# Last node update of a two-layer graph kernel placed in the build banks, ahead of the last batch's products, with the end's loads begun four quads early

## The chip, the core and the metric

The kernel runs on one core of one Trainium2 chip. The metric is the device time of one execution in microseconds (us); the time before is the median of three runs. The core has a matrix engine (PE), a vector engine (DVE), a scalar engine (ACT), a general engine (POOL) and a queue-only engine (SP). SP, ACT and POOL issue DMAs. Each engine works through its own list in order, and semaphores join the lists.

## What is computed

Two graph layers over 6250 nodes with 64 features and 206250 edges sorted by destination. Cut to what matters:

```python
h = jnp.maximum(_layernorm(x, axis=-1), 0.0)
# layer 0: per edge relu([h[src], edge_attr] @ W1 + b1) @ W2 + b2, summed by dst;
#          per node relu([h, sum] @ U1 + c1) @ U2 + c2
x = x + _L0_gnn_ref(h, edge_index, edge_attr_64, ...)
h = jnp.maximum(_layernorm(x, axis=-1), 0.0)
# layer 1: segment_sum(h[src] * edge_weight, dst)
x = x + _L1_gnn_ref(h, edge_index, edge_weight)
```

## The kernel before, in words

**Groups.** The edges are cut into 202 groups of 1024. The main loop (fast_groups, one copy on each engine, all in the same steps s) does two things with group s. It sums layer 0: POOL gathers the rows, PE multiplies the edge features, DVE and ACT add and relu, PE sums by destination (sum_hid), and DVE adds the window to the node sums (add_sums, semaphore acc_added). And it builds layer 1's weighted adjacency as tiles: PE multiplies one-hot matrices into the two build banks pair[2] and pair[3] (build_tile), and ACT copies them into the tile buffer (keep_tiles, semaphore pair_kept). Two groups are a batch (101 batches, 0 to 100), four a quad (51 quads, 0 to 50; the last has one batch). SP stores each batch's tiles in HBM (store_adjacency). The last chunk's columns go to a tensor of their own, tail.

**Node update.** The nodes are ten chunks of 625. When a chunk's layer-0 sums are complete, PE makes g (make_g, two halves), ACT relus it (relu_g), PE makes the update (make_up), DVE adds it (add_up) and normalises it again with ACT's help (centre, square, variance, root, stage_h2; semaphore h2_staged). Chunk 9's sums are complete only with group 201, the last. Before, all of its steps go through mid_bank, a bank that late products share.

**Products.** Layer 1 multiplies the updated nodes h2 by the adjacency. direct(b, half) does it for batch b from the tiles in SBUF, with the chunks that are ready. ACT copies the result (keep_partial, semaphore direct_kept) and SP stores it in partial. late() does the same from pieces read back out of HBM (late_piece), through mid_bank, and DVE adds them up (keep_late) for SP to store (store_late). What is left over, chunk 9 for every quad and chunk 8 too for quads 36 to 46, is done at the end (fast_end).

**The end.** SP loads per quad the sum so far (load_partial, L644, 96 KB, into s_back) and a piece of 480 KB from tail (load_piece, L651) or from adjacency (L653). s_back has four slots: the load of quad q+4 waits until DVE has used quad q (u_kept). The ten slots for pieces lie in the tile buffer. PE multiplies a quad (multiply, L1266 and L1272), DVE adds the sum (keep_u, L1671), PE transposes it (turn_u, L1280), ACT copies, PE places it among the nodes (put, L1290), DVE adds (L1692). After every five quads PE turns a finished chunk (turn_sums, L1298), and it is written out.

**Order.** It is written by hand in each engine's loop. Before, PE does in step 201 direct(99, 1) and the last two late products, in step 202 direct(100, 0) and g's first half, in step 203 direct(100, 1) and g's second half, and in step 204 make_up. SP waits in fast_end, before the first load, for all stores of all kinds.

A float32 matmul is two passes in the profile, so its count there is twice that in the program's order.

Of the kernel before, what the change touches and what calls it, by code (L numbers as in the profile page):

```python
# [15 lines left out]
D = 64  # L16
# [5 lines left out]
NP = 125  # L22
BLK = 5
CN = NP * BLK
BC = BLK * D
# [91 lines left out]
def build(nc, x, src, dst, edge_attr, edge_weight, w1, b1, w2, b2, u1, c1, u2, c2, out):  # L117
# [79 lines left out]
        return sum(ready_for(i) > 0 for i in range(b + 1))  # L197

    ENDS = QUADS + 1

    def groups_of(q):

# [36 lines left out]
    with ExitStack() as ctx:  # L239
# [141 lines left out]
        sum_bank = mid_bank[:, 2 * QCOLS:2 * QCOLS + 2 * W]  # L381
        build_pair = [pair[2], pair[3]]
        assert max(SPLIT * NP, BC, 2 * QCOLS) <= 2 * QCOLS and 2 * QCOLS + 2 * W <= 512
        end_bank = [pair[3][:, 1, 0:2 * COLS], pair[3][:, 0, 0:2 * COLS]]
        turn_bank = [pair[2][:, 0, 0:2 * P], pair[0][:, 1, 0:2 * P]]
        add_bank = [pair[2][:, 1, 0:2 * WB], pair[0][:, 0, 0:2 * WB]]
# [182 lines left out]
        def _(sp):  # L569
# [67 lines left out]
            def store_late(n, q):  # L637
                sp.wait_ge(late_kept, n + 1)
                sp.dma_start(sums_of(2 * q, 2), late_sum[n % BACK]).then_inc(late_stored[n % BACK], 16)

            def load_partial(q):
                wait_count(sp, u_kept, q - SLOTS + 1)
                n = len(batches_of(q))
                sp.dma_start(s_back[:, q % SLOTS, 0:n * COLS], sums_of(2 * q, n)).then_inc(s_loaded[q % SLOTS], 16)  # L644

            def load_piece(q, n, c):
                slot, many = n % PIECES, groups_of(q)
# [12 lines left out]
            def fast_groups():  # L660
                for g in range(SLOTS):
                    load_ea(g, g % TWO)
                for s in range(GROUPS + 4):
# [12 lines left out]

            def fast_end():
                sp.wait_ge(direct_kept, direct_upto(BATCHES - 1))
                for half in range(STAGE // 2):
                    pairs = range(half, BATCHES, STAGE // 2)  # L680
                    sp.wait_ge(adj_stored[half], 16 * sum(has_body(b) for b in pairs))
                    sp.wait_ge(tail_stored[half], 16 * len(pairs))
                for s in range(2):
                    n = direct_upto(BATCHES - 1)
                    sp.wait_ge(s_stored[s], 16 * sum(i % 2 == s for i in range(1, n + 1)))
                for s in range(BACK):
                    sp.wait_ge(late_stored[s], 16 * len(range(s, len(LATE_STEP), BACK)))
                for q in range(ENDS):
                    load_partial(q)
                    for i, c in enumerate(chunks_left(q)):  # L690
                        load_piece(q, FIRST_PIECE[q] + i, c)

            def store_t2(c, slot):
                wait_step(sp, h2_staged, c)
# [121 lines left out]
        def _(act):  # L816
# [99 lines left out]
            def relu_g(c, half):  # L916
                cols = (0, SPLIT * NP) if half == 0 else (SPLIT * NP, CN)
                act.wait_ge(g_made, 2 * c + half + 1)
                wait_count(act, up_made, c)
                act.activation(t_stage[0:D, 0, cols[0]:cols[1]], mid_bank[0:D, 0:cols[1] - cols[0]],  # L920
                               ACT.Relu).then_inc(g_staged, 1)

            def clear_sums(c):
# [5 lines left out]
            def fast_groups():  # L929
                act.wait_ge(table_turned, 20)  # L930
                keep_turned_ea(0, 0)
                keep_turned_ea(1, 1)
                for s in range(GROUPS + 6):
# [12 lines left out]
                    for c in range(CHUNKS):  # L946
                        if s == SUMMED[c]:
                            relu_g(c, 0)
                        if s == SUMMED[c] + 1:
                            relu_g(c, 1)  # L950
                        if s == SUMMED[c] + 2:
                            clear_sums(c)
                        if s == SUMMED[c] + 3:
                            square(2)(c, 0)
                        if s == SUMMED[c] + 4:
                            root(2)(c, 0)

            def keep_turned(q):
                n = len(batches_of(q)) * P
# [44 lines left out]
        def _(pe):  # L1004
# [192 lines left out]

            def make_g(c, half):
                cols = (0, SPLIT * NP) if half == 0 else (SPLIT * NP, CN)
                if half == 0:  # L1200
                    wait_count(pe, late_kept, late_by(SUMMED[c]))
                    pe.wait_ge(acc_added, min(SUMMED[c] + 1, GROUPS))
                    wait_count(pe, x1_made, c)
# [1 line left out]
                    pe.wait_ge(g_staged, 2 * c + 1)  # L1205
                    pe.wait_ge(acc_added, min(SUMMED[c] + 2, GROUPS))
                for w, of in ((u1_deg, beside), (w2u_twice, sums1)):
                    last = pe.matmul(mid_bank[0:D, 0:cols[1] - cols[0]], w[:, :],
                                     of[:, c * CN + cols[0]:c * CN + cols[1]], start=(w is u1_deg),
                                     stop=(w is w2u_twice))  # L1210
                last.then_inc(g_made, 1)

            def make_up(c):
                pe.wait_ge(g_staged, 2 * c + 2)
                pe.wait_ge(acc_added, min(SUMMED[c] + 3, GROUPS))
                for b in range(BLK):
                    last = pe.matmul(mid_bank[0:NP, b * D:(b + 1) * D], t_stage[:, 0, b * NP:(b + 1) * NP],
                                     u2_s[:, :], start=True, stop=True)
                last.then_inc(up_made, 1)

            def fast_groups():
# [4 lines left out]
                for s in range(GROUPS + 6):  # L1226
# [14 lines left out]
                    b = s // 2 - 1  # L1241
                    if 0 <= b < BATCHES and ready_for(b):
                        direct(b, s % 2)
                    late(s)
                    for c in range(CHUNKS):
                        if s == SUMMED[c]:
# [6 lines left out]
            def multiply(q):  # L1253
                bank, many = end_bank[q % 2], groups_of(q)
                wait_count(pe, u_kept, q - 1)
                for i, c in enumerate(chunks_left(q)):
                    n = FIRST_PIECE[q] + i
                    slot = n % PIECES
# [119 lines left out]
        def _(dve):  # L1378
# [254 lines left out]
                        dve.tensor_copy(to, of).then_inc(late_kept, 1)  # L1633

            def fast_groups():
                for s in range(GROUPS + 6):
                    if 1 <= s <= GROUPS:
                        add_sums(s - 1)
                    if s < GROUPS:
# [14 lines left out]
                    for c in range(CHUNKS):  # L1654
# [4 lines left out]
                            variance(2)(c, 0)  # L1659
                        if s == SUMMED[c] + 5:  # L1660
                            stage_h2(c, 0)

            def keep_u(q):

# [123 lines left out]
```

## Time and profile before

| what | us |
|---|---|
| median of 3 runs | 2261.81 |
| lowest, highest run | 2261.12, 2263.18 |
| the profiled execution's own time | 2270.83 |
| its span, first to last instruction | 2269.0 |
| PE, DVE, POOL, ACT busy in the span | 1797.8, 1632.2, 1613.5, 842.8 |
| mean granted clock of PE | 0.931 of full |

The profiled execution takes 1.83 us more than its span, and 9.0 us more than the median of the runs. Times inside the trace are microseconds from the span's start. "The chain" is the chain of work that ended last, followed back from the last instruction.

### The profile page before, as it was taken

How to read it: one execution, taken by the hardware profiler on the slowest of the kernel's cores; microseconds unless marked ns; L12 is line 12 of the kernel's file. 1: busy time of each engine (PE TensorE's matmuls, PEld its weight loads, DVE VectorE, ACT ScalarE, POOL GpSimd, SP SyncE). 2: the span in 40 equal slices, each digit the busy share in tenths (PEclk: the TensorE clock that was granted, in tenths of full speed). 3: DMA queues.
4: the chain of work that ended last, by engine and by line, in shares of the span. 5: the costliest groups of instructions: out<-in, count | busy, mean ns of one | idle time of the engine just before them, and what ended most of it. 6: DMA issues, size and time to landing. Idle time of an engine off the chain costs nothing.

```text
span 2269.0 us, 52026 instructions
## 1 busy us (share of the span) xinstructions
PE 1797.8 (79%) x19448; PEld 1527.7 (67%) x19448; DVE 1632.2 (72%) x4933; ACT 842.8 (37%) x1470; POOL 1613.5 (71%) x1671
## 2 busy tenths in 40 slices
PE   6766576767677777778778877888888899999898
PEld 6555455655565666567667766776777788788787
DVE  7876677767776777777777777777777677877564
ACT  5333343434343434333343333434334333433211
POOL 7777777777777777777777777777777777777200
PEclk9988889878998999899989999999999999999999
DMA  4355556555764676378548755875876588578798
GB/s 104 113 179 178 179 176 204 185 172 173 241 208 137 197 249 209 112 232 255 187 129 260 247 159 165 255 227 156 248 234 197 170 268 257 154 218 255 228 304 278
DMA packets 375605, 459.58 MB, mean 203 GB/s; under 512 B 77256, under 2 KB 297688, under 8 KB 371766
## 3 DMA queue, kind: packets, MB, share of 16 engines
q1 hardware_dynamic: 317274, 401.51, 53.7%
q0 software_dynamic: 51776, 53.07, 10.3%
q8 instruction: 160, 2.62, 0.5%
q10 hardware_dynamic: 6300, 1.60, 0.3%
q14 instruction: 95, 0.78, 0.1%
HBM read 281.45 MB, written 174.54 MB: 201 GB/s over the span
## 4 chain that ended last, share of the span: by engine, by line
POOL 67%; issue 21%; PE 8%; DMA 3%; DVE 1%; ACT 0%; SPq 0%; POOLq 0%
POOL rows L780 67%; PE pair L1266 2%; PE pair L1046 1%; DMA stage<-tail 1%; DMA late_piece<-adjacency 1%; PE pair L1162 1%; PE pair L1290 1%; PE pair L1180 1%; PE pair L1147 1%; PE pair L1280 1%; DMA stage<-adjacency 0%; PE pair L1034 0%; PE pair L1298 0%; DMA rows<-table,idx 0%; PE pair L1272 0%
## 5 line engine op out<-in xcount | busy, mean ns | idle before, releaser
L780 POOL DMA_INDIRECT rows<-table,idx x1616 | 1574.2, 974 | 494.6 <-issue 492.4
L906 ACT COPY stage<-pair 128x600 f32<-128x600 f32 x808 | 538.7, 667 | 882.3 <-PE pair L1147 837.7
L1147 PE MATMUL pair<-bld 128*128 128x300 bf16 x4848 | 757.6, 309 | 5.7 <-DVE bld L1599 5.6
L1147 PEld LDWEIGHTS pair<-bld 128*128 128x128 bf16 x4848 | 549.0, 118 | 140.9 <-issue 14.0
L1599 DVE TENSOR_SCALAR bld<-iota_key,key 128x300 bf16<-128x300 f16 x1616 | 583.0, 361 | 78.1 <-PE pair L1147 75.9
L1609 DVE TENSOR_TENSOR bld<-bld,part 128x512 bf16<-128x512 bf16 x1212 | 481.6, 397 | 0.0
L1107 PE MATMUL pair<-w1b,rings 128*128 128x128 f32 x1616 | 258.2, 310 | 253.3 <-DVE rings L1575 252.9
L1575 DVE TENSOR_TENSOR rings<-rows,pair 128x512 f32<-128x512 f32 x202 | 138.9, 688 | 427.9 <-DMA rows<-table,idx 424.4
L1107 PEld LDWEIGHTS pair<-w1b,rings 128*128 128x128 f32 x1616 | 227.6, 216 | 289.0 <-DVE rings L1575 286.6
L1180 PE MATMUL pair<-late_piece,h 125*64 125x192 f32 x1856 | 201.9, 337 | 117.2 <-issue 104.6
L1162 PE MATMUL pair<-stage,h 125*64 125x96 f32 x4230 | 234.8, 253 | 0.2 <-issue 0.2
L1180 PEld LDWEIGHTS pair<-late_piece,h 125*64 125x64 f32 x1856 | 133.4, 138 | 138.7 <-issue 132.2
L1162 PEld LDWEIGHTS pair<-stage,h 125*64 125x64 f32 x4230 | 204.9, 140 | 0.7 <-issue 0.6
L896 ACT ACTIVATE rings<-rings 128x512 f32<-128x512 f32 x202 | 127.6, 632 | 191.4 <-DVE rings L1575 191.3
L1602 DVE TENSOR_TENSOR bld<-iota_lo,lo 128x512 bf16<-128x512 f16 x404 | 161.7, 400 | 0.0
L1592 DVE TENSOR_REDUCE hot_sum<-hot 128x40 f32<-128x320 f32 x202 | 156.6, 775 | 7.0
L1134 PE MATMUL pair<-hot,rings 128*64 128x40 f32 x3232 | 136.2, 233 | 24.5 <-DVE x_all L1614 23.9
L1134 PEld LDWEIGHTS pair<-hot,rings 128*64 128x64 f32 x3232 | 112.6, 139 | 59.7 <-issue 59.7
L1100 PE MATMUL pair<-ident,rings 128*128 128x128 f32 x808 | 125.7, 280 | 2.5 <-issue 1.7
L892 ACT COPY rings<-pair 128x512 f32<-128x512 f32 x202 | 118.9, 588 | 10.8 <-PE pair L1100 10.7
L1100 PEld LDWEIGHTS pair<-ident,rings 128*128 128x128 f32 x808 | 102.7, 146 | 7.5 <-issue 2.0
L1579 DVE TENSOR_TENSOR hot<-iota,rel 128x320 f32<-128x320 f32 x202 | 98.9, 490 | 0.0
(155 smaller groups left out, 1120.8 us busy)
## 6 DMA issues: line engine op xcount, KB each, us to landing
late_piece<-adjacency SPq DMA_DIRECT2D x232, 480.0 KB
rings<-in_edge_attr_dram SPq DMA_DIRECT2D x202, 256.0 KB
adjacency<-stage SPq DMA_DIRECT2D x14, 2160.0 KB
rows<-table,idx POOLq DMA_INDIRECT x1616
tail<-stage SPq DMA_DIRECT2D x101, 240.0 KB
stage<-tail SPq DMA_DIRECT2D x50, 480.0 KB, 5.8
adjacency<-stage SPq DMA_DIRECT2D x10, 1920.0 KB
adjacency<-stage SPq DMA_DIRECT2D x10, 1680.0 KB
```

The source lines that it names most:

```text
L780: pool.indirect_dma_start(out=rows[:, slot, t, :], out_offset=None, in_=table, in_offset=bass.IndirectOffsetOnAxis(ap=idx[:, g, t:t + 1], ...
L906: act.copy(tiles[:, g % STAGE, :, 2 * j * WT:2 * (j + 1) * WT].rearrange("p h (o w) -> p o h w", w=WT), build_pair[i % 2][:, :, 0:KEYS].re ...
L1100: last = pe.transpose(bank[:, a * P:(a + 1) * P], ea_ring[:, slot, a * P:(a + 1) * P], ident[:, :])
L1107: last = pe.matmul(bank[:, a * P:(a + 1) * P], eaT[:, slot, a, :], w1b2[:, :], start=True, stop=True)
L1134: pe.matmul(half_of(sum_bank, t)[:, 0:W], hid[:, slot, t, 0:D], hot[:, slot, t, :], start=(t < 2), stop=(t >= T - 2))
L1147: last = pe.matmul(build_pair[i // 2 % 2][:, t % 2, 0:KEYS], hot_w[q % 2][k][:, :, u], hot_key[q % 2][:, u, :], start=(k == 0), stop=(k == ...
L1162: last = pe.matmul(half_of(u_bank, h), h2[:, h * D:(h + 1) * D], tiles[0:NP, slot:slot + 2, h, :], start=(h < 2), stop=(h >= many - 2))
L1180: pe.matmul(half_of(mid_bank, h)[:, at:at + QCOLS], h2[:, (c * BLK + h) * D:(c * BLK + h + 1) * D], held[:, :, h, :], start=(h < 2), stop= ...
L1592: dve.tensor_reduce(hot_sum[:, g % TWO, :], hot[:, g % TWO, :, :].rearrange("p t w -> p w t"), AX_X, ALU.add).then_inc(hot_summed, 1)
L1599: return dve.tensor_scalar(hot_key[q % 2][:, u, :], iota_key[:, :], key[:, g, t + u:t + u + 1], None, ALU.is_equal)
L1602: dve.tensor_tensor(hot_eq[q % 2], iota_lo[:, :, :], over(lo[:, g, t:t + 4], P), ALU.is_equal).then_inc(eq_made, 1)
L1609: dve.tensor_tensor(hot_w[q % 2][k], hot_eq[q % 2], over(part[k][:, g, t:t + 4], P), ALU.mult)
```

## The change

It concerns the last three steps and the end. The update of chunk 9 no longer goes through mid_bank but through pair[2], a build bank, and it is written into step 201 on PE: both halves of g straight after direct(99, 1), then direct(100, 0), make_up, direct(100, 1) and only then the two late products. DVE takes the update before the last two keep_late, ACT takes keep_partial(100) after root. On SP the one wait for all stores is split up: for the first four quads it waits for the stores of odd batches and the quad's own sum, loads them ahead of the stores of batch 100's and the last late sums, and then waits quad by quad. The pieces rotate by five slots, so that the first five lie where batch 99's tiles were and not batch 100's.

```diff
+        final_g = [pair[2][:, 0, :], pair[2][:, 1, :]]
+        final_up = pair[2][:, 0, :]
...
+            def piece_slot(n):
+                return (n + PIECES // 2) % PIECES
...
             def load_partial(q):
                 wait_count(sp, u_kept, q - SLOTS + 1)
+                if q < QUADS and late_of[q]:
+                    n = late_of[q][-1]
+                    sp.wait_ge(late_stored[n % BACK], 16 * (n // BACK + 1))
...
             def fast_end():
-                sp.wait_ge(direct_kept, direct_upto(BATCHES - 1))
-                for half in range(STAGE // 2):
...
+                final = BATCHES - 1
+                store_adjacency(final)
+                store_partial(final - 1)
+                tiles_stored((final - 1) % 2)
+                for q in range(AHEAD):
+                    load_quad(q)
+                store_partial(final)
+                for n, c, q in LATE_AT[GROUPS - 1]:
+                    store_late(n, q)
+                tiles_stored(final % 2)
+                for q in range(AHEAD, ENDS):
+                    load_quad(q)
...
+                relu_g(FINAL, 0)
+                relu_g(FINAL, 1)
+                clear_sums(FINAL)
+                square(2)(FINAL, 0)
+                root(2)(FINAL, 0)
+                keep_partial(BATCHES - 1)
...
             def make_g(c, half):
                 cols = (0, SPLIT * NP) if half == 0 else (SPLIT * NP, CN)
-                if half == 0:
+                to = final_g[half] if c == FINAL else mid_bank
+                if c == FINAL:
+                    pe.wait_ge(pair_kept, TILES // 2)
+                    pe.wait_ge(acc_added, GROUPS)
+                elif half == 0:
...
+                    if s == GROUPS - 1:
+                        make_g(FINAL, 0)
+                        make_g(FINAL, 1)
+                        direct(BATCHES - 1, 0)
+                        make_up(FINAL)
+                        direct(BATCHES - 1, 1)
                     late(s)
...
+                add_sums(GROUPS - 1)
+                add_up(FINAL, final_up[0:NP, 0:BC])
+                centre(2)(FINAL, 0)
+                variance(2)(FINAL, 0)
+                stage_h2(FINAL, 0)
+                many = len(LATE_AT[GROUPS - 1])
+                keep_late(GROUPS - 1, 1 if many == 3 else 0, many)
```

FINAL is chunk 9, AHEAD is 4, ENDS is 51.

PE's list before, from the end of direct(99, 1) to the end of make_up. The x23 row is direct(99, 1), L1180 and L1185 are the two late products, L1162 direct(100, ...), L1208 g, L1217 make_up; pair1 holds mid_bank:

```order
L1162 MATMUL pair1<-stage,h2 64x96 x23
L1180 MATMUL pair1<-late_piece,h2 64x192 [waits h2_staged,acc_added,late_loaded0,x1_made,late_kept]
L1180 MATMUL pair1<-late_piece,h2 64x192 x3
L1185 MATMUL pair1<-late_piece,h2 64x96 x2
L1180 MATMUL pair1<-late_piece,h2 64x192 [waits late_loaded1,h2_staged]
L1180 MATMUL pair1<-late_piece,h2 64x192 x3
L1185 MATMUL pair1<-late_piece,h2 64x96 x2
L1162 MATMUL pair1<-stage,h2 64x96 [waits direct_kept,h2_staged,pair_kept]
L1162 MATMUL pair1<-stage,h2 64x96 x21
L1208 MATMUL pair1<-nodes,u1_deg 64x375 [waits x1_made,acc_added,late_kept]
L1208 MATMUL pair1<-nodes,w2u_twice 64x375
L1162 MATMUL pair1<-stage,h2 64x96 x23
```

The same place of PE's list in the changed kernel, from direct(99, 1) to the first late product (there L1193 is direct, L1243 g, L1253 make_up, L1211 a late product):

```order
L1193 MATMUL pair1<-stage,h2 64x96 x23
L1243 MATMUL pair2<-nodes,u1_deg 64x375 [waits acc_added,pair_kept]
L1243 MATMUL pair2<-nodes,w2u_twice 64x375
L1243 MATMUL pair2<-nodes,u1_deg 64x250 [waits acc_added,pair_kept]
L1243 MATMUL pair2<-nodes,w2u_twice 64x250
L1193 MATMUL pair1<-stage,h2 64x96 [waits direct_kept,h2_staged,pair_kept]
L1193 MATMUL pair1<-stage,h2 64x96 x21
L1253 MATMUL pair2<-u2_s,t_stage 125x64 [waits acc_added,g_staged]
L1253 MATMUL pair2<-u2_s,t_stage 125x64 x4
L1193 MATMUL pair1<-stage,h2 64x96 x23
L1211 MATMUL pair1<-late_piece,h2 64x192 [waits h2_staged,acc_added,late_loaded0,x1_made,late_kept]
```

The update moved ahead of batch 100's second half and of both late products, into another bank and without the wait for late_kept; no instruction came or went.

SP's list before, from the last store of tiles to the first loads of the end (L639 store_late, L614 store_partial, L644 and L651 the loads of a quad):

```order
L608 DMA tail<-stage 128x2x240 [waits pair_kept]
L614 DMA partial<-stage 128x96 [waits direct_kept]
L639 DMA partial<-late_own 128x192 [waits late_kept]
L639 DMA partial<-stage 128x192 [waits late_kept] x2
L614 DMA partial<-stage 128x96 [waits direct_kept]
L644 DMA bld<-partial 128x192 [waits late_stored0,s_stored1,late_stored1,s_stored0,late_stored2,tail_stored1,late_stored3,adj_stored1,late_stored4,tail_stored0,late_stored5,adj_stored0,direct_kept]
L651 DMA stage<-tail 128x960
```

SP's list at the same place in the changed kernel (L614 is now the tiles' store, L620 store_partial, L660 and L667 the loads of a quad, L645 store_late):

```order
L614 DMA tail<-stage 128x2x240 [waits pair_kept]
L620 DMA partial<-stage 128x96 [waits direct_kept]
L660 DMA bld<-partial 128x192 [waits late_stored4,tail_stored1,adj_stored1]
L667 DMA stage<-tail 128x960
L660 DMA bld<-partial 128x192 [waits late_stored5]
L667 DMA stage<-tail 128x960
L660 DMA bld<-partial 128x192 [waits late_stored0]
L667 DMA stage<-tail 128x960
L660 DMA bld<-partial 128x192 [waits late_stored1]
L667 DMA stage<-tail 128x960
L620 DMA partial<-stage 128x96 [waits direct_kept]
L645 DMA partial<-late_own 128x192 [waits late_kept]
```

Four quads' loads moved ahead of the last four stores.

## Rows read from the trace of the kernel before

**Rows 1.** The page: the whole chain by engine.

```profile
POOL 67%; issue 21%; PE 8%; DMA 3%; DVE 1%; ACT 0%; SPq 0%; POOLq 0%
```

**Rows 2.** The chain in order of time, 2128 to 2160: start, length, what.

```profile
2132.28 0.87 PE pair L1180 x8
...
2135.66 0.62 PE pair L1208 x2
...
2136.77 1.98 PE pair L1162 x44
2138.76 0.86 PE pair L1208 x4
...
2140.07 1.32 PE pair L1217 x10
...
2141.41 0.50 DVE x_all L1614
...
2158.67 0.80 PE pair L1266 x8
2159.47 0.17 PE pair L1272 x4
```

**Rows 3.** Timeline of PE, 2129 to 2170: start, length, operation [idle before, releaser].

```profile
2131.18 0.85 PE L1180 MATMUL pair<-late_piece,h 125*64 125x192 f32 x8
...
2145.39 1.55 PE L1266 MATMUL pair<-stage,h 125*64 125x192 f32 x8 [4.02 <-DVE h L1404]
...
2156.84 0.87 PE L1266 MATMUL pair<-stage,h 125*64 125x192 f32 x8 [1.63 <-DMA stage<-tail]
...
2160.37 0.87 PE L1266 MATMUL pair<-stage,h 125*64 125x192 f32 x8
...
2162.14 0.87 PE L1266 MATMUL pair<-stage,h 125*64 125x192 f32 x8
...
2164.95 0.87 PE L1266 MATMUL pair<-stage,h 125*64 125x192 f32 x8
```

**Rows 4.** Windows: length, busy PE, PEld, DVE, ACT, POOL, then clock, DMA share, GB/s.

```profile
2132.00:2134.00 2.00, 1.73 (x29) 1.38 (x26) 0.62 (x2) 0.00 (x0) 0.00 (x0) 1.00 0.69 217
...
2136.00:2138.00 2.00, 2.00 (x39) 1.70 (x39) 0.00 (x0) 0.48 (x1) 0.00 (x0) 1.00 0.02 3
...
2146.00:2148.00 2.00, 1.97 (x16) 1.34 (x14) 0.65 (x3) 0.00 (x0) 0.00 (x0) 0.50 1.02 374
```

**Rows 5.** Timeline of SP's queue: when a DMA was issued.

```profile
2131.69 0.32 SPq L614 DMA_DIRECT2D partial<-stage  x1
...
2141.31 0.42 SPq L651 DMA_DIRECT2D stage<-tail  x1
...
2148.10 0.43 SPq L651 DMA_DIRECT2D stage<-tail  x1
...
2158.66 0.43 SPq L651 DMA_DIRECT2D stage<-tail  x1
```

**Rows 6.** L651's landings: 2140 to 2212, then issues of 2141.3, 2148.1, 2149.95.

```profile
DMA to landing us min/median/max: 3.3/5.4/6.7
DMA to landing us min/median/max: 3.3/3.3/3.3
DMA to landing us min/median/max: 4.5/4.5/4.5
DMA to landing us min/median/max: 6.7/6.7/6.7
```

**Rows 7.** Timeline of DVE: the last late sums, the first quad's sum.

```profile
2133.36 0.74 DVE L1629 TENSOR_TENSOR stage<-pair,stage 128x192 f32<-128x192 f32 x2 [3.29 <-PE pair L1185]
...
2147.35 0.36 DVE L1671 TENSOR_TENSOR bld<-pair,bld 128x192 f32<-128x192 f32 x1 [1.38 <-PE pair L1272]
```

**Rows 8.** PE's waits from 2129 on, and the chain at quad 36.

```profile
PE pair L1266 <- DMA stage<-tail: 2.1, 3, 1.6
...
2218.62 1.99 PE pair L1266 x19
```

More of the change, by code:

```diff
@@ L199, in build @@
     ENDS = QUADS + 1
+    FINAL = CHUNKS - 1
+    AHEAD = 4
+    assert SUMMED[FINAL] == GROUPS and SUMMED[FINAL - 1] + GAP + 2 <= GROUPS and ready_for(BATCHES - 1)
+    assert AHEAD <= SLOTS and AHEAD <= PIECES // 2
     def groups_of(q):
@@ L639, in store_late @@
                 sp.dma_start(sums_of(2 * q, 2), late_sum[n % BACK]).then_inc(late_stored[n % BACK], 16)
+            def piece_slot(n):
+                return (n + PIECES // 2) % PIECES
             def load_partial(q):
                 wait_count(sp, u_kept, q - SLOTS + 1)
+                if q < QUADS and late_of[q]:
+                    n = late_of[q][-1]
+                    sp.wait_ge(late_stored[n % BACK], 16 * (n // BACK + 1))
+                else:
+                    for b in batches_of(q):
+                        i = direct_upto(b)
+                        sp.wait_ge(s_stored[i % 2], 16 * ((i + 1) // 2))
                 n = len(batches_of(q))
@@ L646, in load_piece @@
             def load_piece(q, n, c):
-                slot, many = n % PIECES, groups_of(q)
+                slot, many = piece_slot(n), groups_of(q)
                 wait_count(sp, piece_used, n - PIECES + 1)
@@ L662, in fast_groups @@
                     load_ea(g, g % TWO)
-                for s in range(GROUPS + 4):
+                for s in range(GROUPS):
                     if s % 2 == 0 and 2 <= s <= GROUPS:
@@ L675, in fast_groups, with load_quad, tiles_stored @@
                         load_late(n, c, q, q not in LATE_QUAD[:n])
-            def fast_end():
-                sp.wait_ge(direct_kept, direct_upto(BATCHES - 1))
-                for half in range(STAGE // 2):
[L680 to L691, printed above, removed]
+            def load_quad(q):
+                load_partial(q)
+                for i, c in enumerate(chunks_left(q)):
+                    load_piece(q, FIRST_PIECE[q] + i, c)
+            def tiles_stored(half):
+                pairs = range(half, BATCHES, STAGE // 2)
+                wait_count(sp, adj_stored[half], 16 * sum(has_body(b) for b in pairs))
+                sp.wait_ge(tail_stored[half], 16 * len(pairs))
+            def fast_end():
+                final = BATCHES - 1
[10 more added lines that the diff above has]
+                    load_quad(q)
             def store_t2(c, slot):
@@ L919, in relu_g @@
                 wait_count(act, up_made, c)
-                act.activation(t_stage[0:D, 0, cols[0]:cols[1]], mid_bank[0:D, 0:cols[1] - cols[0]],
+                of = final_g[half] if c == FINAL else mid_bank
+                act.activation(t_stage[0:D, 0, cols[0]:cols[1]], of[0:D, 0:cols[1] - cols[0]],
                                ACT.Relu).then_inc(g_staged, 1)
@@ L932, in fast_groups @@
                 keep_turned_ea(1, 1)
-                for s in range(GROUPS + 6):
+                for s in range(GROUPS):
                     if s < GROUPS:
@@ L1207, in make_g @@
                 for w, of in ((u1_deg, beside), (w2u_twice, sums1)):
-                    last = pe.matmul(mid_bank[0:D, 0:cols[1] - cols[0]], w[:, :],
+                    last = pe.matmul(to[0:D, 0:cols[1] - cols[0]], w[:, :],
                                      of[:, c * CN + cols[0]:c * CN + cols[1]], start=(w is u1_deg),
@@ L1215, in make_up @@
                 pe.wait_ge(acc_added, min(SUMMED[c] + 3, GROUPS))
+                to = final_up if c == FINAL else mid_bank
                 for b in range(BLK):
-                    last = pe.matmul(mid_bank[0:NP, b * D:(b + 1) * D], t_stage[:, 0, b * NP:(b + 1) * NP],
+                    last = pe.matmul(to[0:NP, b * D:(b + 1) * D], t_stage[:, 0, b * NP:(b + 1) * NP],
                                      u2_s[:, :], start=True, stop=True)
@@ L1225, in fast_groups @@
                 make_q(0, 0, q_bank)
-                for s in range(GROUPS + 6):
+                for s in range(GROUPS):
                     if s < GROUPS:
@@ L1257, in multiply @@
                     n = FIRST_PIECE[q] + i
-                    slot = n % PIECES
+                    slot = (n + PIECES // 2) % PIECES
                     pe.wait_ge(piece_loaded[slot], 16 * (n // PIECES + 1))
@@ L1635, in fast_groups @@
             def fast_groups():
-                for s in range(GROUPS + 6):
+                for s in range(GROUPS):
                     if 1 <= s <= GROUPS:
```

## Prediction, made before the changed kernel ran

> **What bounds the kernel now.** I read the page first, then the chain in order of time, then each engine's timeline from 2128 us on. The page says that the chain is POOL's gathers for two thirds of the span [rows 1]. The change touches nothing there: the gathers are over by 2132 (POOL's column is 0.00) [rows 4], and every list is the same up to direct(99, 1). So only the last 138 us can move, and the reader should see three things in them.
>
> First, the road to chunk 9's update. direct(99, 1) gives way to the late products at 2131.18 [rows 3]. The DVE addition of the update starts at 2141.41 [rows 2]. Between them lie 10.2 us of PE work in a row, of which the update needs only part. Second, the gap behind it: PE's first multiply of the end starts at 2145.39 after 4.02 us of idleness, and it is slow, 1.55 us for eight passes where later ones take 0.87 [rows 3]. The granted clock is 0.50 there, PE's lower level of 1.2 GHz, and was 1.00 at 2136 [rows 4]. Third, the DMA engines have almost nothing to do at 2136 to 2138 (share 0.02) [rows 4], because SP's first load of a piece goes out at 2141.31 only [rows 5]. Then they are full, and quad 5's piece comes late: PE stands for 1.63 us at 2156.84 [rows 3].
>
> After that the end is PE's. A quad takes 1.77 us (2160.37 to 2162.14) and one with turn_sums 2.81 (2162.14 to 2164.95), so a run of five takes 9.9 us and one quad 1.98 on average [rows 3]. All of its waits for tail pieces sum to 2.1 us, of which the one at quad 5 is 1.6 [rows 8].
>
> **The update's move.** PE now takes from 2131.2: g's first half, four passes at 0.31 (0.62 for two) = 1.24; the second half, 0.86 for four; direct(100, 0), 44 passes, 1.98 by the other half's row; make_up until DVE can add, 2141.41 - 2140.07 = 1.34 [rows 2]. The sum is 5.42, so DVE adds at 2136.6 instead of 2141.41: **4.8 us** earlier. What it has to wait for is there: its two semaphores stand for the last copy of a build bank and the last add_sums, and both follow products that stand ahead of direct(99, 1), which alone is longer than either. g's relus on ACT (0.48 us for the larger half, ACT's column at 2136 [rows 4]) lie beside direct(100, 0); without that cover the second would cost up to 0.48.
>
> From the addition to the first multiply it is 3.98 us (2145.39 - 2141.41), a chain of small DVE and ACT steps that stays as it is [rows 2, 3]. So h2 is there at 2140.6. PE is not idle meanwhile: after make_up (ten passes, issued by about 2136.3) come direct(100, 1) with 2.0 us and two late products of 1.1 us each, together 4.2, to 2140.5 (2132.28 - 2131.18 = 1.10 [rows 2, 3]). They cost nothing, because the chain of h2 covers them to within 0.1 us; if it did not, each would cost its 1.1. ACT's copy of batch 100's product now stands behind root and ends beside the two DVE steps that h2 needs after root, hidden too. On DVE the last late sums (0.74 us) now stand between h2 and the memset of the pads [rows 7]; for that and a small step behind it I put 0.65, an estimate from the 0.36 of the three-times smaller sum of a quad. They end at about 2142.0, and the sum of quad 0 can start there. By itself it could have started at 2141.8, when its multiply is over, so this costs 0.2 us.
>
> **The clock.** The idleness of 4.0 us is gone. In this trace the clock fell only behind it; 1.63 us of idleness at 2156.84 did not lower it (0.87 before and after) [rows 3]. So I take the first quads at the full rate: 0.97 us for quad 0 (0.80 + 0.17 [rows 2]), 1.24 for quad 1 with its transpose, which I put at 0.27, and 1.77 for each from quad 2 on.
>
> **The loads.** SP reaches the first load right after the store of 2131.69 [rows 5], so at 2132.1. All four quads are issued by 2136, when the DMA share is 0.69 and then nearly nothing [rows 4]. Even with the longest landing of 6.7 us [rows 6] quad 0's piece is there at 2139.2, before 2140.6. Four of the quads are thus paid in idle time. What is queued behind them on SP are four stores: they wait for direct_kept (about 2140) and late_kept (about 2141.5) and are out before 2142. Quad 4's load needs u_kept of quad 0, at 2142.5, so it is not held up. It is issued at 2142.9, 2.3 us after the first multiply.
>
> What is late next is quad 4. PE could start it 5.75 us after the first multiply. It starts at 2.3 + L4, where L4 is its piece's time to landing. Quad 8 then starts 1.82 + L8 after quad 4, where 1.82 is the time from a quad's multiply to the issue of the load that it lets go (2156.84 to 2158.66 [rows 3, 5]), or 4 x 1.77 = 7.08 after it if PE is slower. Before, quad 8 starts 2162.14 - 2145.39 = 16.75 after the first multiply. L4 is not in the trace. The nearest rows are 3.3 us for a first load on empty queues, 4.5 for quad 4 of before, 6.7 for one behind others [rows 6]. I take 4.5, since in the new kernel too a few small stores are in front of it. For L8 I take the median, 5.4. Quad 4 starts at 6.8 and quad 8 at 14.0, **2.75 us** earlier than by the old start. It holds the clock's part and the wait's part together.
>
> As to quad 4 the Trainium skill would have it otherwise. Its page "DMA: Bandwidth & Descriptors", section "Anatomy of one DMA — SWDGE (gpsimd) path", fits a DMA as about 2.0 us and the bytes at 436 GB/s. That is an estimate of 3.4 us for the 576 KB of a quad, though for another path than SP's; the first load of before, 3.3 us, agrees, while the 6.7 behind others does not. By it quad 4 would not wait at all, which is the rival "no wait" below.
>
> From quad 8 on everything is the old course, shifted, with quads 36 to 46 (two pieces each) too. Pieces in other slots move no more bytes, and I cost them nothing.
>
> **Sum.** 4.8 + 2.75 = 7.5 us. The profiled span would go from 2269.0 to 2261.5, and its own time from 2270.83 to 2263.3. None of this hangs on the profiler, so the median goes from 2261.81 to **2254.3 us**.
>
> **Rivals.**
> *Queue takes it back.* Both loads take 6.7 us: quad 4 starts at 9.0, quad 8 at 9.0 + 1.82 + 6.7 = 17.5, 0.8 later than by the old start. 4.8 - 0.8 = 4.0, so 2257.8. For it speaks that quad 5's load, issued while the first four were still arriving, took that long; against it, that the first four are now in before quad 4 is asked for.
> *No wait.* L4 is at most 3.45 us, L8 at most 5.26; PE alone sets quad 8, at 0.97 + 1.24 + 6 x 1.77 = 12.8. The gain is 3.9 + 4.8 = 8.7, so 2253.1. The first load of before with its 3.3 us speaks for it, the median 5.4 against it.
> *It doesn't do what it says.* The update is issued early but held, by the last copy of a build bank or by the late products that now fill PE up to h2. If the first multiply comes only 1 us earlier, what is left is that and the clock and load parts: 3.7, so 2258.1. The order of the lists speaks against it.
> *The ring of four turns too slowly.* PE now runs ahead without the old pauses. If landings grow, each round of four quads lasts 1.82 + L instead of 4 x 1.98 = 7.9. That decides from L = 6.1. With eight rounds from quad 4 to quad 36, and 2218.6 - 2145.4 = 73.2 us for that stretch before [rows 3, 8], a mean L of 7.0 gives 9.3 + 8 x 8.82 = 79.9. That is 6.7 lost against 4.8 gained: 2263.7, slower than before. From L = 6.8 it is slower at all. No single landing in the trace is above 6.7, and the change adds no bytes.
>
> **How the numbers follow.** Forecast 0.62, queue takes it back 0.13, no wait 0.19, doesn't do what it says 0.03, ring too slow 0.03. A measurement of this kernel can tell about 0.2% from no change, 4.5 us, so the bounds are 2257.3 and 2266.3. Faster: forecast, no wait and a little of the first rival, 0.82. Same: the rest of it, the third, and part of the fourth, 0.16. Slower 0.02. The range reaches from "no wait" to "queue takes it back", with half a microsecond beyond each for the runs' own spread (2261.12 to 2263.18): 2252.4 to 2258.3.
>
> **What would show it.** In the new trace: g in front of direct(100, 0) at about 2131.2; the addition of the update about 4.8 us earlier, counted from the last build product; no idleness above 1 us ahead of the first multiply, and 0.87 us for its eight passes at clock 1.00; loads from just after the store of batch 99's sum; a wait of about 1 us at quad 4 and nearly none at quad 5; the ninth quad's multiply 14.0 us after the first. The prediction is wrong if the first multiply is less than 4 us earlier, if the clock stays at 0.50 there, or if the end from quad 8 on is no longer the old one shifted, say with waits for pieces that sum to more than 3 us.

## The result, and the profile after

| | before | changed |
|---|---|---|
| median of 20 runs each, us | 2263.38 | 2257.16 |
| lowest, highest | 2259.59, 2268.59 | 2253.26, 2264.06 |
| ratio, 95% interval | 1 | 0.9973 (0.9966 to 0.9981) |
| span of the profiled execution | 2269.0 | 2253.2 |
| last group's sum to the end of the span | 140.27 | 131.70 |

The change gains 6.2 us, 4.3 to 7.7 by the interval (0.0019 and 0.0034 of 2263.4). The two spans differ by far more, 15.8 us. So I count from here on from one point in each trace, the start of the last group's sum on PE (the last L1134 product of before, at 2128.73, and L1165 after). Up to it the changed kernel is 7.2 us shorter, behind it 8.6. The timeline of PE in the changed kernel (start, length, operation, idleness before it and what ended it), from the sum to quad 8:

```profile
2121.50 0.67 PE L1165 MATMUL pair<-hot,rings 128*64 128x40 f32 x16
...
2133.35 0.87 PE L1308 MATMUL pair<-stage,h 125*64 125x192 f32 x8 [0.27 <-DVE h L1446]
...
2139.73 0.87 PE L1308 MATMUL pair<-stage,h 125*64 125x192 f32 x8 [0.47 <-DMA stage<-tail]
...
2142.12 0.87 PE L1308 MATMUL pair<-stage,h 125*64 125x192 f32 x8 [0.56 <-DMA stage<-tail]
...
2147.43 0.87 PE L1308 MATMUL pair<-stage,h 125*64 125x192 f32 x8
```

The first multiply comes 11.85 us after the sum, where before it came 2145.39 - 2128.73 = 16.66 after it. It takes 0.87 us where it took 1.55, and PE stood for 0.27 us where it stood for 4.02 [rows 3]. Quads 4 and 5 wait for their pieces, 1.03 us together, and quad 8 starts 14.08 us after the first multiply.

The road there, by the chain in order of time. It answers [rows 2]: g (L1243), half of direct(100) (L1193), make_up (L1253), the other half, and on another view DVE's addition:

```profile
2124.16 1.83 PE pair L1243 x7
...
2128.09 1.23 PE pair L1253 x10
2129.33 2.04 PE pair L1193 x45
```

```profile
2129.36 0.49 DVE L1656 TENSOR_TENSOR x_all<-x_all,pair 125x320 f32<-125x320 f32 x1 [6.52 <-PE pair L1253]
```

SP's timeline shows the loads' new place, which answers [rows 5]. The store of batch 99's sum, the first piece 1.3 us behind it, and quad 4's piece:

```profile
2124.46 0.32 SPq L620 DMA_DIRECT2D partial<-stage  x1
...
2125.72 0.43 SPq L667 DMA_DIRECT2D stage<-tail  x1
...
2135.38 0.43 SPq L667 DMA_DIRECT2D stage<-tail  x1
```

The windows around the first multiply (columns as in [rows 4]: length, busy engines, clock, DMA share, GB/s) have the clock at 1.00, its upper level, throughout:

```profile
2132.00:2134.00 2.00, 1.73 (x25) 1.57 (x23) 1.54 (x6) 0.42 (x2) 0.00 (x0) 1.00 0.91 353
2134.00:2136.00 2.00, 2.00 (x28) 1.68 (x25) 1.91 (x8) 0.37 (x1) 0.00 (x0) 1.00 0.59 199
```

And PE's waits from 2125 on, which answer [rows 8]: 1.0 us for tail pieces in all, where before had 2.1.

```profile
PE pair L1308 <- DMA stage<-tail: 1.0, 2, 0.6
...
PE pair L1308 <- DVE h L1446: 0.3, 1, 0.3
PE pair L1308 <- DMA stage<-adjacency: 0.2, 1, 0.2
```

### The profile page after: what moved, and what is told of

The parts are those of the page before. It is cut to its first block, busy times and chain, and to the rows that moved or that the text cites. A ratio compares the mean times of both kernels' runs of the same rounds, so it can differ in the third digit from the quotient of the medians.

```text
span 2253.2 us, 52069 instructions
## 1 busy us (share of the span) xinstructions
PE 1788.3 (79%) x19448; PEld 1525.7 (68%) x19448; DVE 1638.4 (73%) x4933; ACT 842.4 (37%) x1470; POOL 1605.6 (71%) x1671
## 4 chain that ended last, share of the span: by engine, by line
POOL 65%; issue 21%; PE 10%; DMA 4%; DVE 1%; SPq 0%; ACT 0%; POOLq 0%
POOL rows L804 65%; DMA late_piece<-adjacency 2%; PE pair L1308 2%; PE pair L1193 1%; PE pair L1178 1%; PE pair L1211 1%; DMA stage<-tail 1%; PE pair L1077 1%; PE pair L1332 1%; PE pair L1322 1%; DMA stage<-adjacency 0%; PE pair L1340 0%; PE pair L1065 0%; PE pair L1165 0%; PE pair L1138 0%
## 5 line engine op out<-in xcount | busy, mean ns | idle before, releaser
L804 POOL DMA_INDIRECT rows<-table,idx x1616 | 1566.3, 969 | 494.6 <-issue 492.3
L1178 PEld LDWEIGHTS pair<-bld 128*128 128x128 bf16 x4848 | 547.8, 118 | 136.9 <-issue 12.9
L1211 PE MATMUL pair<-late_piece,h 125*64 125x192 f32 x1856 | 206.7, 343 | 120.6 <-issue 100.9
L1211 PEld LDWEIGHTS pair<-late_piece,h 125*64 125x64 f32 x1856 | 136.8, 141 | 142.6 <-issue 139.6
L1193 PE MATMUL pair<-stage,h 125*64 125x96 f32 x4230 | 233.1, 252 | 0.0
L1193 PEld LDWEIGHTS pair<-stage,h 125*64 125x64 f32 x4230 | 203.5, 139 | 0.2
L1165 PE MATMUL pair<-hot,rings 128*64 128x40 f32 x3232 | 135.4, 233 | 26.2 <-DVE x_all L1656 26.1
L1165 PEld LDWEIGHTS pair<-hot,rings 128*64 128x64 f32 x3232 | 111.8, 138 | 61.1 <-issue 61.1
```

The lines of the kernel that those rows point to most:

```text
L804: pool.indirect_dma_start(out=rows[:, slot, t, :], out_offset=None, in_=table, in_offset=bass.IndirectOffsetOnAxis(ap=idx[:, g, t:t + 1], ...
L1165: pe.matmul(half_of(sum_bank, t)[:, 0:W], hid[:, slot, t, 0:D], hot[:, slot, t, :], start=(t < 2), stop=(t >= T - 2))
L1178: last = pe.matmul(build_pair[i // 2 % 2][:, t % 2, 0:KEYS], hot_w[q % 2][k][:, :, u], hot_key[q % 2][:, u, :], start=(k == 0), stop=(k == ...
L1193: last = pe.matmul(half_of(u_bank, h), h2[:, h * D:(h + 1) * D], tiles[0:NP, slot:slot + 2, h, :], start=(h < 2), stop=(h >= many - 2))
L1211: pe.matmul(half_of(mid_bank, h)[:, at:at + QCOLS], h2[:, (c * BLK + h) * D:(c * BLK + h + 1) * D], held[:, :, h, :], start=(h < 2), stop= ...
```

## The experiments

All runs but the last (the third of the ring of six) were on chips on which the main loop took 820 to 880 us longer than above, in the kernel before as well (3145 instead of 2263 us), so that their ratios are wide. The gathers are not longer there (962 ns on average in the changed kernel's second trace, against 974 in the trace of before), but the mean granted clock of PE is lower, 0.81 against 0.93, and the chain runs over PE for half of the span. Why the clock is lower, no run told. The stretch behind the last group's sum was not touched by it: the changed kernel's first multiply is at 11.85 or 11.86 us in each of its four profiles, the one above among them. So the verdicts rest on positions in that stretch, one profile each, in us:

| kernel | sum to first multiply | first multiply to quad 8 | sum to the end |
|---|---|---|---|
| before, three profiles | 16.66, 17.16, 17.64 | 16.75, 15.65, 17.48 | 140.27, 140.14, 141.92 |
| changed, four profiles | 11.85, 11.86, 11.85, 11.85 | 14.08, 14.72, 14.57, 13.97 | 131.70, 132.69, 133.78, 131.85 |
| update only | 18.81 | 17.09 | 142.07 |
| loads only | 15.99 | 14.80 | 136.23 |
| loads only, gap filled | 16.31 | 14.06 | 136.76 |
| changed, through mid_bank | 12.70 | 14.12 | 133.34 |
| changed, ring of six, three profiles | 11.86, 11.86, 11.85 | 13.40, 12.90, 12.91 | 127.89, 127.50, 127.55 |

### The update without the early loads

The changed kernel with SP's old end:

```diff
-                for q in range(AHEAD):
-                    load_quad(q)
-                store_partial(final)
...
+                for s in range(BACK):
+                    sp.wait_ge(late_stored[s], 16 * len(range(s, len(LATE_STEP), BACK)))
+                for q in range(ENDS):
+                    load_partial(q)
```

> The changed kernel with SP's old end: PE, ACT and DVE take the update early, but SP waits for all stores before the first load, as before. Positions are counted from the start of the last group's sum (the last L1134 product of before, 2128.73 in its trace). Theory (the loads have to come early too, or the update's move is lost): the last late sums are now at about 12.5 us, their stores are issued by 13 and landed 2 us later, so the first load of a piece goes out at about 15 and lands 3.3 us later: the first multiply of the end comes at 18.5 us instead of 16.7 of before, behind 6 us of idleness of PE with the clock at its lower level. The end is 1 to 2 us longer than before, in all about 2264 where before is 2262.5. Rival (the update's road alone bounds the start of the end): the first multiply at 11.9 us and a gain of 4 to 5 us.

Measured: ratio 1.001 (0.999 to 1.003), and the first multiply 18.81 us after the sum. The timelines of SP (the last store, the first piece) and PE:

```profile
3015.19 0.44 SPq L620 DMA_DIRECT2D partial<-stage  x1
3017.20 0.32 SPq L660 DMA_DIRECT2D bld<-partial  x1
3017.57 0.43 SPq L667 DMA_DIRECT2D stage<-tail  x1
```

```profile
3021.14 1.54 PE L1300 MATMUL pair<-stage,h 125*64 125x192 f32 x8 [7.23 <-DMA stage<-tail]
```

h2 is ready early, but SP waits for the last stores to land, 2.0 us from the last issue, and the piece takes 3.3 more. PE stands for 7.23 us. The rival falls: without the loads the update's move gains nothing, and its end is 0.2 to 1.9 us longer than those of the kernel before.

### The loads without the update

The kernel before with the new fast_end, load_partial and piece_slot on SP, and the rotated slots on PE:

```diff
-                    slot = n % PIECES
+                    slot = (n + PIECES // 2) % PIECES
```

> The kernel before with SP's new end (four quads' loads early, quad by quad waits, pieces rotated by five); PE, ACT and DVE keep their old order. Theory: the first multiply stays at 16.7 us from the last group's sum, still behind 4.0 us of idleness and at the lower clock. Quad 4 and quad 5 no longer wait (1.63 us at quad 5 before), so quad 8 comes 15.1 us after the first multiply where before has 16.75: a gain of 1.6 to 2.1 us. Rival (the old course of the end is set by something else than late pieces, such as the clock): no gain, 0 to 0.5 us.

Measured: ratio 0.9995 (0.9977 to 1.0012). PE's first multiply and its waits for the rest of the span:

```profile
3035.56 1.55 PE L1285 MATMUL pair<-stage,h 125*64 125x192 f32 x8 [4.03 <-DVE h L1423]
```

```profile
PE pair L1285 <- DVE h L1423: 4.0, 1, 4.0
...
PE pair L1317 <- DVE nodes L1711: 0.4, 1, 0.4
PE pair L1285 <- DMA stage<-adjacency: 0.3, 1, 0.3
```

The idleness of 4.03 us and the slow first multiply stay, and not one tail piece is waited for. Quad 8 comes 14.8 us after the first multiply, as expected (15.1). The end is 3.9 to 5.7 us shorter than in the kernel before, more than the 1.6 to 2.1 I gave. Two things were missing in that sum. The later waits of before go too. And the first multiply comes at 15.99 us, not at the 16.7 I expected: before is late there, by 0.7 us in its first trace, and this edit changes nothing on PE ahead of it. That share is not the loads' gain; the section on the two kernels run again shows where it lies.

### The gap filled

The loads-only kernel with products that nobody reads in PE's idle time:

```diff
             def fast_end():
+                for _ in range(13):
+                    pe.matmul(pair[2][:, 0, 0:P], ident[:, :], ident[:, :], start=True, stop=True)
                 pe.wait_ge(twice_made, 1)
```

> The loads-only kernel (update in its old place, four quads' loads early) with 13 products of the identity with itself put on PE between make_up and the first multiply, into a bank that nobody reads; they fill most of the 4.0 us in which PE stood. They add nothing to the output. Theory (what the first quads lost was the clock, and the clock fell for the idleness): the granted clock stays at 1.00, the first eight passes take 0.87 us instead of 1.55, and the fourth quad starts 4.1 us after the first multiply instead of 6.0; the end is 1.5 to 2 us shorter than in the loads-only kernel (136.2 us from the last group's sum), if quads 4 and 5 don't wait instead. Rival (the first quads are slow for cold data or for their long waits on DVE): 1.55 us and 6.0 us again.

Measured: ratio 0.9986 (0.9965 to 1.0007). PE's timeline, with the filling products in the first row, and the window of the first multiply:

```profile
3014.96 3.12 PE L1323 MATMUL pair<-ident 128*128 128x128 f32 x26
3019.15 0.87 PE L1285 MATMUL pair<-stage,h 125*64 125x192 f32 x8 [1.07 <-DVE h L1425]
```

```profile
3018.00:3020.00 2.00, 0.93 (x14) 0.88 (x15) 1.32 (x4) 0.26 (x1) 0.00 (x0) 1.00 0.00 0
```

With the gap filled the clock stays at 1.00 and eight passes take 0.87 us. The fourth quad (quad 3) starts 4.07 us after the first multiply where the unfilled kernel has 5.96: 1.9 us, as expected, and the rival falls. In the loads-only kernel the window before the first multiply had stood at 0.50. But the end is no shorter, 136.76 against 136.23. PE now comes to quad 4 before its piece, stands there for 0.73 us, and 0.85 us more at later quads; quad 8 has kept 0.74 of the 1.9. These waits, which the unfilled kernel has not, are 1.6 us together, so in this pair of profiles the ring of four takes back most of what the clock gives. The ends of single executions scatter by as much.

### The update through the old bank

```diff
-        final_g = [pair[2][:, 0, :], pair[2][:, 1, :]]
-        final_up = pair[2][:, 0, :]
+        final_g = [mid_bank, mid_bank]
+        final_up = mid_bank
```

and the waits that a shared bank needs: the second half of g for the relu of the first, the last late products for the update's addition.

> The changed kernel with the last update in its new place on PE, but through mid_bank as before: the second half of g then waits for the relu of the first, and the late products wait for the update's addition. Theory (the order is what counts, the build banks only save one hand-over): the second half of g starts 0.6 to 0.8 us later, the late products don't wait since direct(100, 1) is longer than make_up's way to the addition; the first multiply comes 12.4 to 12.7 us after the last group's sum instead of 11.85. Rival (without the build banks the move is worth nothing): 14 us or more.

Measured: ratio 0.9977 (0.9957 to 0.9998), the first multiply at 12.70 us. PE's second half of g:

```profile
3006.04 0.61 PE L1247 MATMUL pair<-nodes,u_deg 97*64 97x250 f32 x2 [0.66 <-ACT t_stage L945]
```

It waits 0.66 us for the relu of the first half. At the first multiply the banks are worth 0.85 us, the order the other 4.0 to 4.9. The end, 133.34, lies among those of the changed kernel, so there the 0.85 can't be told from scatter.

### The kernel before and the changed one, again

Five more profiles of one or the other, unaltered.

> The changed kernel once more, unaltered, on the same chip as the other three. Theory (the step from the last group's sum to the end is 8.6 us shorter in the two profiles, the rest of their 15.8 us difference is in the gathers on POOL and is scatter of single executions): the ratio is again between 0.9965 and 0.998, and in its profile the part behind the last group's sum is again 131.5 to 132.5 us long, wherever that sum starts. Rival (the change also shortens the part ahead of it): the last group's sum starts at 2121 to 2123 us again and not at 2126 to 2130.

> The changed kernel, unaltered, beside the three others. Theory: first multiply 11.85 us after the last group's sum, the end 131.5 to 133 us, with a wait at quad 4 or 5 that differs from execution to execution (0.5 to 1.6 us); ratio to the kernel before 0.9966 to 0.998. Rival (the gain is smaller in the usual execution than in the profiled one): 134 us or more.

> The kernel before, unaltered, for a second profile: how much does the stretch from the last group's sum to the end scatter by itself? Theory (the waits for late pieces come and go from execution to execution, the rest is fixed): first multiply of the end 16.0 to 16.7 us after the last group's sum, at the lower clock (1.55 us for eight passes), the end 139 to 141 us; against 131.7, 132.7 and 133.8 with the change, a mean gain of 6.5 to 8 us. Rival (the first profile of before was a long one, and the change gains only 4 to 5 us): 137 to 138 us.

> The same once more. Theory: 139 to 141 us, with 1 to 2.5 us of waits for late pieces at other quads. Rival: 137 to 138 us.

> The changed kernel for a fourth profile, on the same chip as the two of the kernel before. Theory: 131.5 to 134 us from the last group's sum to the end, the first multiply after 11.85 us. Rival: outside of that.

Measured: for the changed kernel ratios of 0.9997 (0.9976 to 1.0019) and 0.9972 (0.9954 to 0.9989), two samples of one thing that show how little a ratio tells on these chips. Their last group's sums start at 3000.71, 2991.32 and 2976.25, so these runs can't say whether the part ahead of the sum is shortened. The ends are 131.7 to 133.8 against 140.1 to 141.9, on average 132.5 and 140.8: a gain of **8.3 us** in profiled executions. Several single values missed what was expected: the ratio of 0.9997 (expected 0.9965 to 0.998), two ends of the changed kernel, 132.69 and 133.78 (131.5 to 132.5, and 131.5 to 133), and of the two new ends of before one, 141.92 (139 to 141).

The first multiply of the kernel before scatters, which I had not expected: 16.66, 17.16, 17.64 us. In the third of its profiles PE's timeline has the reason among the late products ahead of the update:

```profile
2954.61 0.87 PE L1180 MATMUL pair<-late_piece,h 125*64 125x192 f32 x8 [1.46 <-DMA late_piece<-adjacency]
```

The last late piece had not landed. In the changed kernel that product stands behind the update, and no profile of it has a wait there.

The first trace of before has a delay at this place too, though no wait is listed. Its second late product starts 1.10 us after the first (2132.28 - 2131.18 [rows 2, 3]); in the loads-only kernel the same two are 0.82 us apart, so 0.28 us of the 1.10 is not work:

```profile
3022.02 0.85 PE L1199 MATMUL pair<-late_piece,h 125*64 125x192 f32 x8
...
3022.84 0.85 PE L1199 MATMUL pair<-late_piece,h 125*64 125x192 f32 x8
```

And its direct(100, 0) takes 2.22 us up to g where that of the loads-only kernel takes 1.86, with a short gap in it:

```profile
2133.97 1.56 PE L1162 MATMUL pair<-stage,h 125*64 125x96 f32 x33 [0.19 <-issue]
```

The second profile of before has the same gap, the third has not; what it is stays open. The two delays account for the scatter to within 0.03 us: 15.99 us without either, 16.66 with 0.28 and 0.36, 17.16 with 0.78 and 0.36, 17.64 with 1.66 and none.

### Six slots for the sums

The changed kernel with RING_END = 6 slots in s_back, u_side, u_turn and place_hot moved up by 384 columns, and five quads loaded early:

```diff
-        s_back = bld[:, 0:SLOTS * 2 * COLS].rearrange("p (s c) -> p s c", s=SLOTS)
+        s_back = bld[:, 0:RING_END * 2 * COLS].rearrange("p (s c) -> p s c", s=RING_END)
...
-                wait_count(sp, u_kept, q - SLOTS + 1)
+                wait_count(sp, u_kept, q - RING_END + 1)
...
-    AHEAD = 4
+    AHEAD = 5
```

> The changed kernel with six slots for the loaded sums instead of four and five quads loaded early. Theory (the two short waits at quads 4 and 5, 0.47 and 0.56 us in the profile of the changed kernel, come from the ring of four, since the load of quad 4 waits for quad 0): both waits go, quad 8 starts 13.0 us after the first multiply instead of 14.1, and the end is 1.0 to 1.5 us shorter than with the change. Rival (DMA is full there, and a longer ring only makes the queue longer): waits of about 1 us stay, at later quads, and the gain is under 0.3 us.

> The changed kernel with six slots for the loaded sums and five quads loaded early, once more. Theory: as in its first profile the end is 128 us from the last group's sum (131.7 and 132.7 with the change alone), 1 us of it before quad 8 and 3 us in the quads with two pieces, and the time is 3 to 5 us below that of the change, so on a chip where the kernel before takes 2263 it takes 2252 to 2254. Rival (the 4 us were scatter of one execution): 131 to 133 us.

> The changed kernel with six slots for the loaded sums and five quads loaded early, for a third time. Theory: the stretch from the last group's sum to the end is 127.5 to 128.5 us again, 12 to 14 us shorter than in the kernel before (140.1 to 141.9), and the time 9 to 13 us below that of the kernel before, 0.9943 to 0.996 of it where that takes 2263 us. Rival (the shorter end is given back before it, or only profiled executions have it): a gain of 4 us or less against the kernel before.

Measured: ratios to the kernel before of 0.9974 (0.9951 to 0.9997), 0.9963 (0.9945 to 0.9981), and, on a chip where that kernel takes 2263.7, **0.9950 (0.9936 to 0.9964)**, a median of 2252.45 us. That is 11.3 us below the kernel before, and 4.7 us below the changed kernel's 2257.16, though the two were not timed side by side. All of PE's waits in the last profile from 2125 on:

```profile
PE pair L1341 <- DVE nodes L1742: 0.4, 1, 0.4
PE pair L1309 <- DVE h L1447: 0.3, 1, 0.3
```

No piece is waited for any more, and quad 8 starts 12.91 us after the first multiply (13.40 in the first profile, with one wait of 0.42). The end is 127.5 to 127.9, 4.9 us shorter on average than with the change. The queue does become longer (one-piece landings with a median of 5.9 to 6.1 us and up to 8.5, against 5.3 to 5.7 and at most 7.0 with four slots), but PE no longer sees it, so the rival, that it only becomes longer, falls. The slots and the fifth early quad were changed together; no run separates them. I had given 1.0 to 1.5 us for the first of these runs, by the waits at quads 4 and 5 alone. More comes from the quads with two pieces. From quad 36 to quad 46 it is 31.9 us before, 31.2 with the change and 28.4 here, by the starts of the first and the last product of that kind (kernel before, changed, ring of six):

```profile
2218.55 2.04 PE L1266 MATMUL pair<-stage,h 125*64 125x192 f32 x20
...
2250.48 2.06 PE L1266 MATMUL pair<-stage,h 125*64 125x192 f32 x20
```

```profile
2203.54 2.10 PE L1308 MATMUL pair<-stage,h 125*64 125x192 f32 x20
...
2234.72 2.02 PE L1308 MATMUL pair<-stage,h 125*64 125x192 f32 x20
```

```profile
2198.69 1.85 PE L1309 MATMUL pair<-stage,h 125*64 125x192 f32 x20
...
2227.10 2.17 PE L1309 MATMUL pair<-stage,h 125*64 125x192 f32 x20
```

Windows over most of that stretch, kernel before and ring of six:

```profile
2218.00:2250.00 32.00, 31.04 (x283) 24.44 (x282) 13.84 (x53) 3.72 (x10) 0.00 (x0) 1.00 1.06 376
```

```profile
2199.00:2227.00 28.00, 28.00 (x280) 22.48 (x276) 13.46 (x52) 3.58 (x10) 0.00 (x0) 1.00 1.07 379
```

The rate is the same, 376 and 379 GB/s, with the DMA share above 1. Six slots let SP begin the two-piece quads two quads sooner, in the time in which PE still has one-piece quads, so fewer bytes are left for this stretch. By these rates 31.9 us move about 12.0 MB and 28.4 us about 10.8, a difference of roughly one two-piece quad (1.08 MB); this is an estimate. The step is read from the lists, and no run isolates it.

## Why the prediction was right

It gave 2254.3 us, that is 7.5 below 2261.8. The median fell by 6.2, and 7.5 is inside the interval (4.3 to 7.7). The time 2257.16 is in the range, 1.1 us from its upper end; 1.6 us of its distance from 2254.3 is that the median of before is higher in 20 runs than in the three I had. The lower end of the range, 2252.4, is 0.7 us below "no wait" and not the half microsecond that the text says; nothing hangs on it.

**The update's move: right.** The addition was to come 4.8 us earlier; it came at 2129.36 - 2121.50 = 7.86 us after the sum, against 2141.41 - 2128.73 = 12.68: 4.82. The sum of 5.42 us from direct(99, 1) to the addition measured about 5.4. The relus, the late products and ACT's copy were hidden as said: PE stood 0.27 us before the first multiply. But the 1.10 us that I took for the length of a late product is 0.82 of work and 0.28 of delay, and direct(100, 0), which I had put at 1.98 by the other half, had 0.36 more before than the loads-only kernel's. Against the loads-only kernel, which has neither, the move is worth 4.1 us (15.99 - 11.85); against the three executions of before it is worth 4.8, 5.3 and 5.8, since those delays are gone from the changed kernel's road: its first multiply repeats to 0.01 us. The 4.8 is right for the trace I had, and I had not seen that 0.6 us of it varies from execution to execution.

**The clock: right**, and now shown by a run: 1.9 us at the fourth quad. The Trainium skill has it likewise (page "TensorE: Matmul & The Clock Gate", section "What's actually happening": the throttled clock is the default, and activity releases it); the 4.03 us of idleness ended at 0.50, the filled one at 1.00.

**The loads: right in sum, and by a range in each execution.** They went out 1.3 us behind the store of batch 99's sum. Quad 4 was to start at 6.8 and quad 8 at 14.0 us; measured 6.38 and 14.08, and 13.97 to 14.72 in the other profiles. For L4 I took 4.5 us; the piece issued at 2135.38 landed after 4.2. I expected a wait at quad 4 and nearly none at 5; there were 0.47 and 0.56, and in other executions 1.5 or 1.6 at the one or the other. Quad 8 itself did not wait: its piece took 4.8 us, not the 5.4 of my formula, and what held quad 8 was quad 5's piece, issued at 2136.33 with 5.7 us to landing, a step that my sum passed over. Quad 4 was 0.4 us earlier than said and the way from it to quad 8 0.5 us longer (7.70 instead of 7.2), so that the single numbers missed and their sum did not. That part of the match is luck.

**"From quad 8 on the old course, shifted": about 1 us short.** From quad 8 to the end it was 2269.0 - 2162.14 = 106.9 before and 2253.2 - 2147.43 = 105.8 after. The other profiles give 107.3 and 106.8 before, 106.1, 107.4 and 106.0 after. So part of it is scatter of later waits. The waits for tail pieces sum to 3.1 us in two of the four executions, which is my sign of being wrong if they are counted from the first quad; behind quad 8, where I meant them, they are 1.6 at most, and 2.2 in one execution if the wait for an adjacency piece is added.

**What the trace could not give.** The profiles gain 8.3 us on average, the timed runs 6.2 (4.3 to 7.7). The difference of about 2 us stays open. The three ends of before lie up to 1.8 us apart and the four of the changed kernel up to 2.1, so scatter can account for it. The 7.2 us ahead of the sum come from the gathers: the last one starts at 2116.9 in the trace of before and at 2109.0 in the changed one, and the 1616 gathers take 1574.2 and 1566.3 us together, the same 7.9 us less. The lists do not differ there. That this is scatter and not the change is likely (the 20 runs of before alone lie 9.0 us apart) but not shown.

**The rivals.** "No wait" (2253.1) is what the ring of six makes of it: quad 8 at 12.9, as that rival's sum says (12.8). "Queue takes it back" would have had quad 8 at 17.5; the highest was 14.72. The ring turned no slower than before. "It doesn't do what it says" falls with the 4.8 us at the first multiply, and even through the old bank it was 4.0.

## What to carry over

Two waits that end together have to be moved together. Against the mean end of before the update alone gave +1.3 us here and the loads alone -4.6, which add up to -3.3; both together gave -8.3. The 5 us between the two is well above the 1 to 2 us by which the ends scatter. After such a move, look at what the first step behind it is fed by. Where a load waits for a use some steps back, the number of slots times the time per step must be more than the landing time plus the time from a use to the issue that it lets go, or a gain ahead of it is partly taken back. Here four slots give 4 x 1.77 = 7.1 us against 5.7 + 1.8 = 7.5 with the landing of quad 5's piece, and PE waited; six give 10.6 against at most 8.5 + 1.8 = 10.3 in the one-piece quads, and it waited once, for 0.42 us, or not at all. Six slots instead of four, with five quads ahead, were worth more (4.9 us) than the clock's whole part (1.9).

## What the runs showed of the hardware

A 480 KB piece with 96 KB in front of it, one per quad, lands in 3.3 to 7.0 us in the kernels with four slots, and which one is late differs from execution to execution of the same kernel. The waits for tail pieces sum to 1.0, 3.1, 3.1 and 1.9 us in four executions of the changed kernel, while the first multiply, which waits for no load there, repeats to 0.01 us.

The DMA rate in the two-piece stretch stood at 376 to 379 GB/s over some 30 us, with four slots (376 before, 378 with the change) and with six (379). The Trainium skill (page "DMA: Bandwidth & Descriptors", section "Specifications") gives about 358 GB/s as the HBM limit of a core; these windows are 5 to 6% above it.
